# First attention of a macaron block: output projection in the free half of the numerators' bank, residual first on VectorE

## The reference

```python
qkv = x @ Wqkv_w.T + Wqkv_b          # x: layer norm of the residual stream
k = k * SCALE
g = sigmoid(gamma_raw)               # one decay per head, 16 heads of 16
def step(state, qkv_t):
    state = g * state + outer(v_t, k_t)
    y_t = state @ q_t
    return state, y_t
x = x + (y @ out_w.T + out_b)
```

## Time and profile before

| | us |
|---|---|
| median of 3 runs | 2599.61 |
| lowest, highest | 2595.66, 2601.04 |
| the profiled execution | 2597.78 |
| its span, first to last instruction | 2595.7 |
| stretch of the first attention (518 to 961) | 443.0 |
| TensorE, VectorE, ScalarE busy in it | 401.1, 324.2, 154.6 |

### The profile page before, as it was taken

One profiled execution on the slowest core, in us unless ns is written; L12 is line 12 of the kernel. 1 busy time (PEld: TensorE's weight loads), 2 busy tenths in 40 slices (PEclk: granted clock), 3 DMA queues, 4 the chain that ended last, 5 costly groups with the idle time before them and its releaser, 6 DMA issues.

```text
span 2595.7 us, 78340 instructions
## 1 busy us (share of the span) xinstructions
PE 2441.3 (94%) x32360; PEld 2136.1 (82%) x32360; DVE 1866.0 (72%) x4374; ACT 1420.4 (55%) x2362; POOL 1284.7 (49%) x1398
## 2 busy tenths in 40 slices
PE   4999999999998989999999999989999999979999
PEld 3888888877877867888888999978888888858998
DVE  8999899577776779999996666545655566646664
ACT  4555555433333325556665788854454454418886
POOL 5878888611111128889996433213434444463332
PEclk9999999999999989999999999999999999989999
DMA  5000000010100010000000000000000000000111
GB/s 187 1 7 1 1 1 1 1 25 22 24 22 21 23 51 1 1 1 1 1 1 1 18 1 2 1 19 17 18 16 17 18 17 16 17 6 26 33 33 41
DMA packets 67728, 46.13 MB, mean 18 GB/s; under 512 B 13216, under 2 KB 66352, under 8 KB 67376
## 3 DMA queue, kind: packets, MB, share of 16 engines
q1 hardware_dynamic: 67376, 41.13, 5.7%
HBM read 15.91 MB, written 8.40 MB: 9 GB/s over the span
## 4 chain that ended last, share of the span: by engine, by line
PE 66%; issue 14%; POOL 11%; DVE 5%; ACT 4%; DMA 0%; SPq 0%; POOLq 0%; DVEq 0%; ACTq 0%
PE ps L46 11%; PE ps L48 11%; PE ps L47 11%; PE ps L1562 5%; PE ps L1560 5%; PE ps L1541 4%; PE ps L1540 4%; PE ps L618 3%; PE ps L270 3%; PE ps L1130 2%; POOL a1pry L2116 2%; POOL a1pry L2118 2%; POOL a1l L2104 2%; PE ps L1161 2%; POOL a1P L2112 2%
## 5 line engine op out<-in xcount | busy, mean ns | idle before, releaser
L1605 DVE TENSOR_TENSOR gHl<-gHf,gHh 128x512 fp32r<-128x512 f32 x256 | 187.2, 732 | 183.6 <-ACT gHh L1581 183.4
L237 POOL TENSOR_SCALAR ve<-mv 128x4 f32<-128x4 f32 x96 | 22.0, 229 | 589.3 <-DVE mv L227 585.1
L46 PE MATMUL ps<-WGH,XTH 128*128 128x512 f32 (+1 forms) x768 | 300.5, 391 | 7.4 <-ACT fSG L687 4.5
L48 PE MATMUL ps<-WGL,XTH 128*128 128x512 f32 (+1 forms) x768 | 290.7, 379 | 0.0
L47 PE MATMUL ps<-WGH,XTL 128*128 128x512 f32 (+1 forms) x768 | 290.2, 378 | 0.0
L687 ACT ACTIVATE fSG<-ps 128x704 f32<-128x704 f32 x128 | 97.0, 758 | 312.7 <-PE ps L48 312.7
L833 POOL TENSOR_TENSOR fHTL<-fHTF,fHTH 128x768 fp32r<-128x768 f32 x128 | 235.9, 1843 | 62.0 <-ACT fHTF L696 62.0
L1560 PE MATMUL ps<-W2T,gHh 128*128 128x256 f32 x1024 | 255.4, 283 | 0.0
L1562 PE MATMUL ps<-W2T,gHl 128*128 128x256 f32 x1024 | 253.0, 281 | 0.0
L2104 POOL TENSOR_TENSOR a1l<-a1l,a1rc 128x128 f32<-128x128 f32 x128 | 49.5, 408 | 364.3 <-DVE a1rc L2071 364.3
L46 PE MATMUL ps<-WDH,fHTH 128*128 128x256 f32 x768 | 221.8, 289 | 2.4 <-issue 2.4
(11 more groups left out here) (248 smaller groups left out, 7150.1 us busy)
## 6 DMA issues: line engine op xcount, KB each, us to landing
X<-in_x SPq DMA_DIRECT2D x16, 512.0 KB, 8.9
a0vp<-a0vt SPq DMA_DIRECT2D x256, 32.0 KB, 2.2
a1vp<-a1vk SPq DMA_DIRECT2D x256, 32.0 KB, 2.1
out<-X SPq DMA_DIRECT2D x16, 512.0 KB, 2.9
tws<-in_w SPq DMA_DIRECT2D x2, 1024.0 KB, 7.8
WN<-in_wgu SPq DMA_DIRECT2D x3, 384.0 KB, 5.5
a0km<-in_wqkv SPq DMA_DIRECT2D x2, 384.0 KB, 3.2
a1pry<-in_aw SPq DMA_DIRECT2D x1, 768.0 KB, 4.5
```

The source lines that it names most:

```text
L46: e.matmul(o, hh, mh, start=first, stop=False)
L48: return e.matmul(o, hh, ml, start=False, stop=last)
L1605: dve.tensor_tensor(Hl[m % 8][:, :], Hf[m % 4][:, :], Hh[m % 8][:, :].bitcast(F32), ALU.subtract).then_inc(s_hl, 1)
```

## The change

Three edits, all in the first attention.

- `slots0` has no slot ("o", n - 2) any more, so the ring holds one place less per tile; `emptied0` loses its entry. All later slots move to other banks and have other predecessors.
- `attn0_out` writes to the right half of bank 6, whose left half holds the numerators. `enter` waits for the residual that reads this half, in addition to its waits of before.
- VectorE does the residual of tile n - 2 ahead of `held(n)`.

```diff
@@ slots0 @@
                 if n < NT:
-                    yield ("v", n)
-                if n >= 2:
-                    yield ("o", n - 2)
-                if n < NT:
-                    yield from [("s", n, q) for q in range(4)]
+                    yield from [("v", n), *[("s", n, q) for q in range(4)]]
                     if n % 8 < 7:
                         yield ("u", n)
@@ emptied0 @@
-                    "u": (s_ss, masked(2 * n + 1)), "o": (s_xd, 64 + n + 1)}[kind]
+                    "u": (s_ss, masked(2 * n + 1))}[kind]
@@ attn0_out @@
-            bank = attn0_take(pe, "o", p)
             pe.wait_ge(s_yl, p + 1)
...
-                t = mm3(pe, bank[:, 0:256], a0YH[:, ks], a0YL[:, ks], a0OH[:, k, :], low[:, :], k == 0, k == 1)
+                t = mm3(pe, PS[6][:, 256:512], a0YH[:, ks], a0YL[:, ks], a0OH[:, k, :], low[:, :], k == 0, k == 1)
@@ enter @@
                 if m:
                     pe.wait_ge(s_yl, m)
+                    pe.wait_ge(s_xd, 64 + m)
@@ attn0_dve @@
-                if n < NT:
-                    held(n)
                 if n >= 2:
...
-                    dve.tensor_tensor(X[:, p, :], bank0("o", p)[:, 0:256], X[:, p, :], ALU.add).then_inc(s_xd, 1)
+                    dve.tensor_tensor(X[:, p, :], PS[6][:, 256:512], X[:, p, :], ALU.add).then_inc(s_xd, 1)
                 if n < NT:
+                    held(n)
                     decay(n)
```

## The result

| us | before | after |
|---|---|---|
| median (4 runs each) | 2597.6 | 2560.7 |
| lowest to highest | 2594.7 to 2601.0 | 2556.0 to 2564.4 |
| span of the profiled execution | 2595.7 | 2557.4 |
| ratio | | 0.9856, 95% interval 0.9834 to 0.9879 |

The kernel became 37 us faster.

What follows compares the result with a forecast made beforehand. TensorE, busy 94% of the span, was taken to bound the kernel. 17.3 + 1.2 + 4.5 - 0.7 = 22.3 us took the profiled 2597.8 to 2575.5; with the median 1.8 higher, 2577 us, range 2571 to 2589.

Steps and rivals of the forecast that it cites:

- The waits of the ring: First attention: score matmuls wait for a bank of the ring of six; taking the output projection out removes these waits.
- 17.3 + 1.2 + 4.5: Score waits saved, us: tiles 3, 7, ... (projection 3), tiles 2, 6, ... (second query pass), tiles 1, 5, ... (second XTL).
- the eight that would go: Eight listed score waits for the second XTL at tiles 1, 5, ... 57, put at 0.44 us each, all saved.
- The added wait: TensorE's enter waits for the residual of the tile before last in bank 6; hidden except behind the last tile.
- a loss at the end alone: Behind the last tile nothing hides enter's wait for the residual, so the stage's end moves: 0.7 us lost.
- the slack of 0.35 to 0.63: Time by which the residual is visible before enter would start: tile 27 0.63, tile 29 0.35, tile 30 0.55 us.
- The wait instructions: TensorE's queue: 52 more at 51 ns each, run ahead of the matmuls, taken as 0; 2.7 us if none covered.
- rival 1: Freed tiles run into TensorE's "issue" pauses before state products, 1.15 us each: 2594 us if all fifteen, 2586 if half; chance 0.17.
- Rival 2: First attention: with fewer gaps the granted clock comes back too, up to 5 us more gain: 2572 us; chance 0.07.

Runs made afterwards that it cites:

- the bank alone: Changed kernel with VectorE's residual again behind values and decayed keys, output projection still in bank 6; 2579.1 us, ratio 0.9935 to the kernel before.
- the kernel with all three waits back: Changed kernel with the scores again waiting for the second XTL, second decayed Q and projection 3; 2599.2 us, ratio 1.0004 to the kernel before.
- the second trace: The changed kernel run once more, same program, for a second trace and more times; 2558.0 us, ratio 0.9869 to the kernel before.
- before + 64: Kernel before with 64 satisfied wait instructions more in TensorE's queue in the first FFN; 2592.8 us, ratio 1.0004 to the kernel before.
- the kernel with the wait without time: Changed kernel with a wait ahead of each tile's scores for the same tile's output projection; 2582.8 us, ratio 0.9946 to the kernel before.
- one wait back: Changed kernel with the scores at tiles 3, 7, ... 59 again waiting for ScalarE's work on projection 3; 2586.2 us, ratio 0.9960 to the kernel before.

## Why the prediction was wrong

*The waits of the ring.* Forecast 17.3 + 1.2 + 4.5 = 23.0 us, measured 22.4, and 0.31 us from turns to scores at every tile but the first two; tile 1 keeps a wait of 0.6 for XTL, which the forecast had counted among the eight that would go. Right but for that.

*The added wait.* Forecast were slack at every steady tile and a loss at the end alone. The trace has enter at its 0.20 in all tiles up to 60. At tile 61 it waits 1.3 us (forecast about 1.4), at tile 62 0.6, and then:

```profile
912.30 0.41 DVE L1297 TENSOR_TENSOR X<-ps,X 128x256 f32<-128x256 f32 x1
...
912.82 0.67 PE L1144 MATMUL ps<-a0qp,a0S 32*32 32x64 f32 x32 [2.27 <-issue]
...
919.18 0.42 DVE L1297 TENSOR_TENSOR X<-ps,X 128x256 f32<-128x256 f32 x1
...
919.71 1.02 PE L1144 MATMUL ps<-a0qp,a0S 32*32 32x64 f32 x32 [0.56 <-issue]
```

The first is hidden: the chain that ended last runs over VectorE and GpSimd there. The last stands on that chain with 0.56, forecast 0.7. Right, and the bank alone shows that the slack of 0.35 to 0.63 was owed to the order: behind the decayed keys it is -0.26.

*The wait instructions.* Forecast were 52 more. The trace has 460 in place of 521: wrong in sign. Enter has 63 wait instructions in both though it waits for one thing more, so the new wait joined the others of its matmul. It had no part in the time, as the kernel with all three waits back shows: its trace has 460 as well, and its time is that of before.

*The pauses.* This is the step that failed: the sum of the forecast has no term for them. They were held to stay as they were ("the stream has nearly the same instructions") and entered only as rival 1, with the wrong sign, as a loss where a freed tile runs into one more. They shrank instead: 15.2 us became 5.6 and, in the second trace, 2.9. The reason given, that pauses come "also at those where the scores never waited", was true of two of the sixteen alone. Fourteen, with 14.6 of the 15.2 us, stood behind the scores of a tile 1, 2 or 3 of a group, where the scores wait; the two in tiles 0, 4, ... were of 0.37 and 0.24 us. The runs showed that the waits bring them: with the waits back in the changed kernel they sum to 14.7 us, and with a wait that costs 0.3 us to 21.4.

*The clock.* Rival 2 had the right sign with a price of up to 5 us. Among the traces with the ring's waits, the rest of the split is 386.5 and 386.2 us without a stretch at half clock, 388.5 and 389.0 with two, 390.1 with three. With the banks and the order of the changed kernel it is 382.7, 382.7 and 383.8 in the traces with none, 382.7 with one, 386.9 with three and 386.4 with four. That is about 1 us each, an estimate, and some 3.6 us of the gain between these two traces. It isn't a steady part: before + 64 had the full clock too, at the time of before. The Trainium skill (TensorE: Matmul & The Clock Gate, "What's actually happening") says that activity releases the throttle. The traces agree in part: half clock begins beside a pause at 797.9 and 927.6 us of before (pauses of 1.28 and 1.04) and 1.8 us behind a wait of the scores at 869.5. But the kernel with the wait without time had 22 pauses of up to 1.33 us and no half clock in this part, so idle time of this size doesn't bring it by itself.

*What stays open.* Of the 7.4 us of the rest, some 3.6 is the clock, and 1.3 are waits of TensorE for decayed keys and the low part of y (0.35, 0.62 and 0.38) in tiles 60 to 63, which are now covered by the waits of enter. About 2.5 us is not accounted for. What asks for a packet of instructions, and so why a wait delays it, is not shown. Why executions of one kernel differ by 8 to 14 us (one wait back: 2578.7 to 2592.7) was not tried; the two traces of the changed kernel differ by 2.7 us in pauses.

## What to carry to other kernels

In this kernel, a wait on TensorE cost more than its idle time where dense small matmuls followed it: the packets of the next instructions started later, and the engine paused behind the wait. So waits ahead of dense work should be for things long done, even if those that come just in time look free; here one such wait per tile, 0.3 us in all, brought 16 to 18 us of pauses. And where two jobs share a bank, look at which of its readers stands first in its queue: the same bank gave 16 us with the old order and 34 to 37 with the new.

## What was not expected of the hardware

- TensorE's instructions come in packets of 256 (258 packets, 66,152 instructions), and in before all idle times at "issue" of this part stand at number 193 or 194 of such a block. In before and after, the block that TensorE paused for began to run 2.3 to 2.9 us after its packet's start. The pauses are up to 1.4 us in these two, and up to 2.0 in the bank-only kernel.
- A wait ahead of each tile's scores that is met just when they could start cost 0.3 us in all, and raised the pauses from 3 to 6 us to 21.4.
- An idle time put down to "issue" can be a wait for another engine (enter for the residual, at 58 places of the bank-only kernel, mostly 0.17 to 0.19 each) or for instructions. In these traces the place in the block of 256 told them apart.
